# Expert rounds of a perceiver layer: tables in turn order, the tail of the down projection on half the rows, and part of its loading on ACT

## The reference

```python
x = x + cross_attention(layernorm(x), ctx_2048, mask)     # 256 tokens x 512, memory of 4096 rows
x = x + self_attention(layernorm(x), w_qkv, w_out, q_gain) # 16 heads of 32, causal, rotary on even heads
# expert layer, on layernorm(x):
router_logits = x @ gate_w                                 # 64 experts
routing_weights, selected = jax.lax.top_k(router_logits, 8)
routing_weights = jax.nn.softmax(routing_weights, axis=-1)
gate = ragged_dot(hidden_sorted, gate_proj_w, group_sizes) # per expert 512 x 192
up   = ragged_dot(hidden_sorted, up_proj_w, group_sizes)   # per expert 512 x 192
down = ragged_dot(silu(gate) * up, down_proj_w, group_sizes) # per expert 192 x 512
out  = sum over the 8 chosen experts of down * routing_weight
```

## Time and profile before

| what | value |
|---|---|
| time, median of 3 runs | 379.88 us (377.63 to 380.1) |
| time of the profiled execution | 380.15 us |
| span of that execution, first to last instruction | 378.4 us |
| PE busy | 323.2 us (85%) |
| DVE, ACT, POOL busy | 166.6, 119.3, 85.3 us |
| rounds (Silu instructions) | 28, in 16 teams |
| first gate and up product | at 149.79 us |

### The profile page before, as it was taken

How to read it: one execution, slowest core, us unless ns; L and a number is a source line. 1 busy time by engine, 2 the same in 40 slices (tenths; PEclk the granted TensorE clock), 3 DMA queues, 4 the chain that set the end, 5 groups by cost and what they waited for, 6 DMA issues and landing times.

```text
span 378.4 us, 9715 instructions
## 1 busy us (share of the span) xinstructions
PE 323.2 (85%) x3092; PEld 184.3 (49%) x3093; DVE 166.6 (44%) x450; ACT 119.3 (32%) x190; POOL 85.3 (23%) x376
## 2 busy tenths in 40 slices
PE   0699999889967524998999999998999999999894
PEld 0554444447743413445555555554654555555462
DVE  7733565945856770133233333333333332333233
ACT  1112202154731401143334433343333433333431
POOL 4000003200000003222243224423342322422320
PEclk9999999995989655799999999999999999999999
DMA  2999959100000039002999805993993999999501
GB/s 60 357 403 408 408 188 377 40 3 0 2 2 0 0 113 388 1 0 76 363 356 382 325 0 185 396 390 112 381 381 153 337 383 392 394 387 396 205 0 55
DMA packets 39743, 83.22 MB, mean 220 GB/s; under 512 B 4648, under 2 KB 12976, under 8 KB 39600
## 3 DMA queue, kind: packets, MB, share of 16 engines
q1 hardware_dynamic: 39312, 82.99, 58.5%
q10 hardware_dynamic: 416, 0.04, 0.1%
HBM read 82.49 MB, written 0.52 MB: 219 GB/s over the span
## 4 chain that ended last, share of the span: by engine, by line
PE 53%; DVE 12%; POOLq 11%; issue 9%; POOL 8%; ACT 4%; DVEq 2%; ACTq 0%
PE psum L1076 12%; POOLq L489 7%; PE psum L1131 6%; PE psum L1109 6%; PE psum L906 4%; PE psum L945 4%; PE psum L918 4%; PE psum L1084 3%; POOL store L496 3%; POOL store L501 3%; POOLq L490 2%; DVE store L728 2%; PE psum L1118 2%; POOL store L505 2%; PE psum L1006 2%
## 5 line engine op out<-in xcount | busy, mean ns | idle before, releaser
L1109 PE MATMUL psum<-store 128*32 128x384 f32 x896 | 80.0, 499 | 0.7 <-ACT store L856 0.7
L1076 PE MATMUL psum<-store 128*128 128x128 bf16 x696 | 45.9, 222 | 18.6 <-DVE store L728 18.2
L1076 PEld LDWEIGHTS psum<-store 128*128 128x128 bf16 x696 | 40.9, 99 | 38.8 <-DVE store L728 25.6
L496 POOL TENSOR_TENSOR store<-store,slot_row 128x64 f32<-128x64 f32 x112 | 29.5, 295 | 123.4 <-issue 120.4
L1131 PE MATMUL psum<-store 128*32 128x256 f32 (+1 forms) x672 | 54.0, 454 | 0.0
L501 POOL TENSOR_TENSOR store<-store 128x64 f32<-128x64 bf16 x112 | 29.5, 295 | 96.5 <-PE psum L1118 95.9
L1109 PEld LDWEIGHTS psum<-store 128*32 128x32 f32 x896 | 29.2, 112 | 39.9 <-issue 34.7
L873 ACT ACTIVATE y_parts<-psum,w_slot 128x512 fp32r<-128x512 f32 x28 | 19.2, 687 | 77.7 <-PE psum L1131 77.7
L1084 PE MATMUL psum<-y_parts,place_T 128*128 128x512 f32 x120 | 36.0, 423 | 4.1 <-DVE y_parts L711 2.5
L868 ACT ACT_TABLE_LOAD x28 | 35.9, 1283 | 7.1 <-issue 6.9
L856 ACT ACTIVATE store<-psum 128x512 f32<-128x512 f32 x29 | 17.3, 598 | 61.2 <-PE psum L1076 61.2
(11 more groups left out here) (207 smaller groups left out, 357.6 us busy)
## 6 DMA issues: line engine op xcount, KB each, us to landing
store<-n_L_ffn_gate_proj_w_dram SPq DMA_DIRECT2D x64, 384.0 KB, 5.7
store<-in_L_ffn_up_proj_w_dram SPq DMA_DIRECT2D x64, 384.0 KB, 6.0
store<-n_L_ffn_down_proj_w_dram SPq DMA_DIRECT2D x64, 256.0 KB, 5.7
store<-n_L_ffn_down_proj_w_dram SPq DMA_DIRECT2D x64, 128.0 KB, 5.9
store<-in_L_attn_w_qkv_dram SPq DMA_DIRECT2D x1, 3072.0 KB, 14.4
store<-in_ctx_dram SPq DMA_DIRECT2D x2, 1024.0 KB, 6.3
store<-in_L_attn_w_out_dram SPq DMA_DIRECT2D x1, 1024.0 KB, 16.5
x_sb<-in_x_dram SPq DMA_DIRECT2D x1, 512.0 KB, 4.3
```

Of the source, the lines that this page charges most:

```text
L496: last = pool.tensor_tensor(apart[:, :, j], over_slots(rank, e), slots, ALU.subtract)
L1076: last = pe.matmul(bank[3][:, c * P:(c + 1) * P], xparts[:, h, part, c, :], pick_t[:, h], start=(k == 0), stop=(k == 3 * TH - 1))
L1109: last = pe.matmul(bank[0][quarter, 0:2 * INTER], xs[:, c, quarter], w[:, :, c, :], start=(c == 0), stop=(c == DC - 1))
```

## The change

- `rank` and `rw` are carried over into turn order by a product with the turn table (`turned`), so POOL does L496 and L501 in one instruction each for a whole team and loads no expert numbers; `slot_no` has the slot numbers of all rounds, so that L505 goes. Teams 0 to 2 use the tables as they are.
- Hidden values of the tail stand once for each half: rows 0 to 63 of the tail's place hold the left columns, rows 64 to 127 the right ones. Down is four groups of products of 256 columns: main left, main right, tail left (rows 0 to 63 of the array), tail right (rows 64 to 127). Left goes to bank 6, right to bank 7. One transpose fewer, and 256 instead of 384 columns to copy to `hidT`.
- The tail is thus two DMAs an expert, five in all. For teams 4 to 15 SP issues four of them, and ACT issues the right tail: after the last round of team q - 4 it loads the expert number from `turns` and issues the DMA, four times, before it goes on to the next team.
- PE takes the rounds of a team out of two packed words by shift and mask, instead of a load for each team.
- One Silu on a single value (`warm`) ahead of the loop.
- Ahead of the loop: clearing is done at the program's start, the subtractions for the bfloat16 parts move from DVE to POOL, the router works by halves of the tokens, the routing weights are computed before the order of the experts, and the first gather takes its own `pick_0` from DVE and runs before the lists are made.

```diff
-        hid = carve([P, 3 * P + 2])
-        hid_tails = hid[:, P:].rearrange("p (h n) -> p h n", h=2)[:, :, 0:P:2]
-        hidT = carve([P, 3, P])
+        hid = carve([P, 2 * P])
+        hid_tails = hid[:, P:].rearrange("p (h n) -> p h n", h=2)
+        hidT = carve([P, 2, P])
...
+        y_half = (psum[:, 6, D // 2:], psum[:, 7, 0:D // 2])
+        y_whole = psum[:, 6:8, :].rearrange("p b n -> p (b n)")[:, D // 2:D // 2 + D]
...
+        def tail_of(lane, e, half):
+            cols = slice(half * (D // 2), (half + 1) * (D // 2))
+            return (lane[half * TAIL_I:(half + 1) * TAIL_I, TAIL_AT:SLOT_W],
+                    down_proj[bass.ds(e, 1), MAIN_I:, cols].rearrange("e r n -> (e r) n"))
...
-                                     (lane[:, TAIL_AT:SLOT_W], down_proj[bass.ds(e, 1), MAIN_I:].rearrange("e r (h n) -> (e r h) n", h=2))):
+                    for dst, src in parts + [tail_of(lane, e, half) for half in range(tails)]:
                         sp.dma_start(dst, src).then_inc(s_w[r], 16)
...
-                load_team(team, r)
+                load_team(team, r, tails=1)
...
-            pool.wait_ge(s_tables, 12)
-            pool.wait_ge(s_cnt, 2)
+            for part, ready, done in ((0, s_xp1, s_xr1), (1, s_xp2, s_xp)):
+                for h in range(TH):
+                    pool.wait_ge(ready, h + 1)
+                    if part == 0:
+                        pool.tensor_tensor(rest[:, h], xn[:, h].rearrange("p (q c) -> p c q", c=DC),
+                                           xparts[:, h, 0], ALU.subtract).then_inc(done, 1)
+                    else:
+                        pool.tensor_tensor(xparts[:, h, 2], rest[:, h], xparts[:, h, 1], ALU.subtract).then_inc(done, 1)
+
+            pool.wait_ge(s_tables, 11)
             pool.wait_ge(s_rk, 1)
             pool.wait_ge(s_rw, 1)
+            pool.wait_ge(s_cnt, 2)
             step = pool.alloc_register("pool_step")
             pool.reg_mov(step, 0)
-            slots = slot_row[:, :].unsqueeze(1).to_broadcast([P, TH, BLK])
-
-            def over_slots(table, e):
-                return table[:, :, bass.ds(e, 1)].to_broadcast([P, TH, BLK])
-
-            with pool.Fori(0, TEAMS) as q:
-                team = [pool.value_load(turns[0:1, bass.ds(q * TEAM + j, 1)], min_val=0, max_val=EXP_N - 1) for j in range(TEAM)]
+
+            def rounds_of(q, table):
                 count = pool.value_load(rounds[0:1, bass.ds(q, 1)], min_val=1, max_val=TOK // BLK)
-                with pool.Fori(0, count):
+                cols = bass.ds(q * TEAM, TEAM)
+
+                def over_slots(t):
+                    return t[:, :, cols].unsqueeze(3).to_broadcast([P, TH, TEAM, BLK])
+
+                with pool.Fori(0, count) as r:
                     v = pool.snap(step)
+                    slots = slot_no[:, bass.ds(r, 1), :].unsqueeze(1).to_broadcast([P, TH, TEAM, BLK])
                     pool.wait_ge(s_pk, v + 1)
-                    pool.wait_ge(s_gpr, v + 1)
-                    for j, e in enumerate(team):
-                        last = pool.tensor_tensor(apart[:, :, j], over_slots(rank, e), slots, ALU.subtract)
-                    last.then_inc(s_ap, 1)
+                    pool.tensor_tensor(apart, over_slots(table[:, 1]), slots, ALU.subtract).then_inc(s_ap, 1)
                     pool.wait_ge(s_pk, v + 2)
                     pool.wait_ge(s_mtp, v + 1)
-                    for j, e in enumerate(team):
-                        last = pool.tensor_tensor(mix_t[:, :, j], pick_t[:, :, j], over_slots(rw, e), ALU.mult)
-                    last.then_inc(s_mx, 1)
-                    for j, e in enumerate(team):
-                        left = rank[:, :, bass.ds(e, 1)]
-                        last = pool.tensor_tensor(left, left, blk_c[:, :, :], ALU.subtract)
-                    last.then_inc(s_gpr, 1)
+                    pool.tensor_tensor(mix_t, pick_t, over_slots(table[:, 0]), ALU.mult).then_inc(s_mx, 1)
                     pool.reg_add(step, step, 1)
+
+            with pool.Fori(0, EARLY) as q:
+                rounds_of(q, rw_rank)
+            pool.wait_ge(s_tn, 1)
+            with pool.Fori(EARLY, TEAMS) as q:
+                rounds_of(q, turned)
...
+                dve.wait_ge(s_lg, h + 1)
+                ch.step(dve.tensor_copy(logits[:, h], bank[h][:, 0:EXP_N]))
+                ch.step(dve.max(top8[:, h], logits[:, h]))
+                dve.tensor_scalar(ntop[:, h:h + 1], top8[:, h, 0:1], -1.0, None, ALU.mult).then_inc(s_tv, 1)
+                ch.step(dve.match_replace(cut[:, h], top8[:, h], logits[:, h], LOWEST))
+                dve.tensor_tensor(chosen_b[:, h], cut[:, h], logits[:, h], ALU.not_equal).then_inc(s_ch, 1)
+
+            dve.wait_ge(s_ch, 2)
+            dve.wait_ge(s_ex, 2)
+            ch.step(dve.tensor_tensor(rexp, rexp, chosen_b, ALU.mult))
+            ch.step(dve.tensor_reduce(rsum[:, :], rexp, AX.X, ALU.add))
+            ch.step(dve.reciprocal(rsum[:, :], rsum[:, :]))
+            dve.tensor_tensor(rw, rexp, rsum[:, :].unsqueeze(2).to_broadcast([P, TH, EXP_N]), ALU.mult).then_inc(s_rw, 1)
+
             dve.wait_ge(s_rank, 1)
-            n_col, n_row = bank[2][0:EXP_N, 0:1], bank[2][0:EXP_N, EXP_N:2 * EXP_N]
+            dve.scalar_tensor_tensor(rank, bank[2][:, 0:TH * EXP_N].rearrange("p (h e) -> p h e", h=TH), 1.0,
+                                     chosen_b, ALU.add, ALU.mult).then_inc(s_rk, 1)
+            dve.wait_ge(s_tables, 11)
+            dve.wait_ge(s_rk, 1)
+            dve.tensor_tensor(pick_0, rank[:, :, 0:TEAM].unsqueeze(3).to_broadcast([P, TH, TEAM, BLK]),
+                              slot_no[:, 0:1, :].unsqueeze(1).to_broadcast([P, TH, TEAM, BLK]), ALU.is_equal).then_inc(s_pk0, 1)
...
-            dve.memset(pick_t, 0.0).then_inc(s_pk, 1)
-            dve.memset(mix_t, 0.0).then_inc(s_mtp, 1)
-            dve.memset(hid, 0.0).then_inc(s_gpr, 1)
-            dve.wait_ge(s_xp2, 2)
-            for h in range(TH):
-                dve.tensor_tensor(xparts[:, h, 2], rest[:, h].rearrange("p (q c) -> p c q", c=DC),
-                                  xparts[:, h, 1], ALU.subtract).then_inc(s_xp, 1)
-
-            dve.wait_ge(s_ex, 2)
-            ch.step(dve.tensor_tensor(rexp, rexp, chosen, ALU.mult))
-            ch.step(dve.tensor_reduce(rsum[:, :], rexp, AX.X, ALU.add))
-            ch.step(dve.reciprocal(rsum[:, :], rsum[:, :]))
-            dve.tensor_tensor(rw, rexp, rsum[:, :].unsqueeze(2).to_broadcast([P, TH, EXP_N]), ALU.mult).then_inc(s_rw, 1)
...
+            dve.tensor_copy(turns[:, :], lists[:, 0:EXP_N]).then_inc(s_cnt, 1)
+            dve.wait_ge(s_cnt, 2)
+            ch.step(dve.scalar_tensor_tensor(spare[:, :], rounds[:, :], -1.0, radix[:, :], ALU.add, ALU.mult))
+            ch.step(dve.tensor_reduce(radix[:, 0:2], spare[:, :].rearrange("p (w q) -> p w q", w=2), AX.X, ALU.add))
+            dve.tensor_copy(packs[:, :], radix[:, 0:2]).then_inc(s_cnt, 1)
...
-                    dve.tensor_copy(hidT, bank[1][:, 0:3 * P].rearrange("p (k s) -> p k s", k=3)).then_inc(s_ht, 1)
+                    dve.tensor_copy(hidT, bank[1][:, 0:2 * P].rearrange("p (k s) -> p k s", k=2)).then_inc(s_ht, 1)
...
+            act.wait_ge(s_flp, 1)
+            act.activation(flipped[0:EXP_N], bank[7][0:EXP_N, :].rearrange("p (a h t) -> p a h t", a=2, h=TH), ACT.Copy).then_inc(s_flc, 1)
             act.wait_ge(s_xg, 1)
             copy_gathered()
+            act.wait_ge(s_tnp, 1)
+            act.activation(turned, bank[6][:, 0:4 * EXP_N].rearrange("p (a h e) -> p a h e", a=2, h=TH), ACT.Copy).then_inc(s_tn, 1)
+            act.wait_ge(s_cnt, 2)
             step = act.alloc_register("act_step")
             act.reg_mov(step, 0)
-            with act.Fori(0, TEAMS) as q:
+            act.activation(warm[:, :], ntop[0:1, 0:1], ACT.Silu).then_inc(s_warm, 1)
+
+            def rounds_of(q):
                 count = act.value_load(rounds[0:1, bass.ds(q, 1)], min_val=1, max_val=TOK // BLK)
                 with act.Fori(0, count):
                     v = act.snap(step)
@@ -870,8 +892,20 @@
                     copy_gathered()
                     act.wait_ge(s_y, v + 1)
                     act.wait_ge(s_ws, v + 1)
-                    act.activation(y_parts[:, 0], bank[6], ACT.Copy, scale=w_slot[:, :]).then_inc(s_yh, 1)
+                    act.activation(y_parts[:, 0], y_whole, ACT.Copy, scale=w_slot[:, :]).then_inc(s_yh, 1)
                     act.reg_add(step, step, 1)
+
+            rounds_of(0)
+            with act.Fori(1, LAPS) as lap:
+                for r in range(RING):
+                    act.wait_ge(s_y, act.snap(step))
+                    for j in range(TEAM):
+                        e = act.value_load(turns[0:1, bass.ds((lap * RING + r) * TEAM + j, 1)], min_val=0, max_val=EXP_N - 1)
+                        dst, src = tail_of(ring[r][:, j], e, 1)
+                        act.dma_start(dst, src).then_inc(s_w[r], 16)
+                    rounds_of(lap * RING + r - EARLY)
```

(57 more changed lines are left out.)

130 lines of the change are left out of this document (60 added, 70 removed).

## The result

The changed kernel takes 400.94 us (median, 400.36 to 401.65) against 378.75 us for the kernel before in the same comparison (372.6 to 380.1): ratio 1.0675, 95% interval 1.0615 to 1.0735. The forecast was 391 us in a range of 375 to 401, so 22 us were lost where 11 were forecast. The sign and the costly part were right; the gains were put too high. The profiled execution of the changed kernel took 401.65 us, with a span of 399.6, against 380.15 and 378.4. Some executions of a kernel take over 1.5% longer than its fastest, at a lower granted clock: the times in this document are medians over all executions, the ratios and their intervals leave those out.

What follows compares the result with a forecast made beforehand. The loop was taken as bound by PE, at team changes by POOL's sequencer. From 380.15 us: -8.7 - 11.5 - 7.3 + 33 + 6 = +11.5, so 391.7; median 0.3 lower, 391 us, range 375 to 401.

Steps and rivals of the forecast that it cites:

- the costly part: ACT's loads and issues of right tails ahead of Silu, at twelve team starts: loss 33 us.
- What bounds the kernel before: Expert loop bound by PE, at team changes by POOL's sequencer, whose lateness makes the gather wait 10.6 us over 15 changes.
- Tables in turn order, -11.5 us: Team changes: POOL's four expert-number loads and L505 go, so the gather's wait goes; gain 11.5 us (10.5 to 12).
- ACT issues the right tails, +33 us: Twelve team starts: four tails at 1.22 us delay Silu to 6.1 us; 2.7 us each reach PE, 33 us lost.
- the half clock, +6: Idle PE of about 2.5 us in those twelve rounds brings half-clock stretches after about half: loss 6 us (0 to 15).
- The "45" of the prediction: Loss at ACT's block if each has one issue stall as long as SP's longest, 1.46 us: 45 us instead of 33.
- PE's round, -0.26 us times 28 = -7.3: Each loop round: one transpose less, 0.11 us, and down 0.15 us shorter with tails side by side; gain 7.3 us.
- Ahead of the loop, -8.7 us: Router to first gate and up: work moved off DVE and POOL starts it at 141.1 instead of 149.8; gain 8.7 us.
- The table load: The 1.28 us load before Silu leaves the loop through the early Silu; gain nothing in rounds of before.
- the rival that priced it at 15 us: Table load stays in the loop, between ACT's issues and Silu: 12 x 1.28 = 15 us more, 406 us; chance 0.05.
- Weights "aren't late": Expert weight loads in the loop: asked for earlier than before, never late, so ACT's issues buy nothing.

Runs made afterwards that it cites:

- experiment 1: The changed kernel with ACT's block of loads and issues deleted, SP issuing all five loads of an expert: 376.82 us, ratio 0.9996.
- experiment 7: The changed kernel with 16 idle products of 256 columns on PE ahead of the wait for hidden values in every round: 421.20 us, ratio 1.122.
- experiment 6: The kernel before, with only ACT issuing its single tail DMA for teams 4 to 15, SP the other three loads: 404.50 us, ratio 1.078.
- experiment 3: The changed kernel with down's order main left, tail left, tail right, main right: 402.62 us, ratio 1.060.
- experiment 8: The changed kernel with the old single tail, all loads on SP, start clears moved to DVE's wait before the rotary part, DVE counts from packed words: 357.76 us.
- experiment 4: The changed kernel without the Silu on `warm` ahead of the loop: 401.26 us, ratio 1.062.
- experiment 11: The changed kernel with old tail layout, late clears, all loads on SP, the tail in two DMAs for partitions 0 to 63 and 64 to 127: 373.99 us.
- the twelfth: The changed kernel with the old single tail, late clears, all loads on SP, gate weights in two DMAs over 128 partitions each: 367.85 us, ratio 0.979.
- experiment 2: The changed kernel with all loads on SP and the tail as before: one DMA, three transposes, down as 512 + 256 + 256 columns: 363.92 us.
- fifth: The kernel of experiment 2, with ACT still doing the wait and four loads of expert numbers but issuing no DMA: 365.39 us, ratio 0.968.

## Why the prediction was right and wrong

- **What bounds the kernel before:** right; POOL's loads vanish from the chain, and the gather's wait with them.
- **Tables in turn order, -11.5 us:** nearly right. Beyond 26 rounds of 7.39 us each, the kernel before spends 12.4 us at its changes of team. The changed one without ACT's block (its other rounds, and the late ones of experiment 1) spends 2.7, so the gain is 9.7 us, and up to 0.9 more lies in the first round and the last.
- **ACT issues the right tails, +33 us, and the half clock, +6:** right. Predicted 1.22 us a tail, measured 1.26; Silu at 6.1 us, measured 5.5 to 6.65; 2.7 us reaching PE, measured 28.4/12 = 2.4; half clock 6 us, by experiment 7 it is 7.7. Together 39 predicted, 38.3 measured (experiment 1); that the sum is so near is in part luck, as the wait is 4.6 us less than forecast, the clock 1.7 more, and 2.2 of the 38.3 us belong to neither. Experiment 6 shows that this part suffices. SP's longest issue, which I took to lie in the loop (1.46 us), is at 24.64 us, during the attentions; in the loop it is 1.31. The "45" of the prediction would be 43.
- **PE's round, -0.26 us times 28 = -7.3:** this is the step that failed. In-team rounds take 7.39 us before and 7.34 to 7.40 after, so the term is 0, or 0.03 us a round at best. Both halves of my reasoning on the array came true, and the sum was still wrong: all eight products of the tails run side by side (they start within 0.05 us), each change of shape costs its 0.11 us (the tails, and in experiment 3 main right behind them, start that much late), and a transpose is gone. What I left out is what PE's sequencer does meanwhile: the loop's end, which the old down had hidden, now stands open for 0.2 to 0.3 us a round. I had noted that down "runs straight into gate and up" and took it for a property of the loop; it was one of the old down. Experiment 3, with 7.15 us a round, is close to the 7.39 - 0.26 = 7.13 that I had forecast: the gain exists, but in another order of the same products. The rule of the Trainium skill's "TensorEngine Tiling (Array Packing)", Tiling Modes, that a change of tiling mode drains TensorE pointed the right way. Neither it nor the 0.11 us that I took for such a drain tells of the sequencer.
- **Ahead of the loop, -8.7 us:** from the layer norm's output to the first gate and up it is 24.3 us before (125.52 to 149.79 on the timeline) and 16.06 after (127.18 to 143.24), a gain of 8.2. The term was right, but the start as a whole gained 6.55, since that output is 1.66 us later. The clears that moved to the start were costed at nothing, and they were not hidden: DVE's lane there is full, so the first layer norm starts at 7.83 instead of 6.56 us, 1.27 later. With the clears elsewhere (experiment 8) it starts at 6.54. The changed kernel:

```profile
1.21 0.27 DVE L541 MEMSET place_T<- 128x256 f32 x1
1.64 0.91 DVE L542 MEMSET y_parts<- 128x1024 f32 x1 [0.16 <-issue]
...
7.83 0.67 DVE L421 BATCH_NORM_STATS2 stats<-x_sb 128x6 f32<-128x512 f32 x1
```

  The first layer norm of the kernel before, on its own timeline:

```profile
6.56 0.67 DVE L402 BATCH_NORM_STATS2 stats<-x_sb 128x6 f32<-128x512 f32 x1
```

  The other 0.4 us are two differences that the change doesn't account for and that nearly cancel: the cross attention took 2.4 us longer in this execution, and the self-attention 2.0 us less, as it has 3.4 us at half clock less than the one before (last section).

- **The table load:** none in the loop, as forecast; but the rival that priced it at 15 us had no ground (experiment 4).
- **Weights "aren't late":** true of the changed kernel, but only because ACT takes part of the issues. I had concluded that issuing from ACT buys nothing; experiment 1 shows that it buys SP's keeping up, as rounds 25 to 27 take 41.5 us there and 28.5 with ACT's issues. And I didn't look at where the two tail loads write, which costs some 10% of the rate (experiment 11).

The miss of 10 us is thus 7.3 of PE's round, 2.1 of the start, 0.9 of the tables, 0.3 outside the span, less 0.7 of the block. Of the 2.1, 1.3 are the clears.

## What to carry to other kernels

A DMA issue is an instruction of the engine that issues it: with the load of its address it took 1.26 us here, and four of them ahead of the first operation that other engines wait for cost 38 us in twelve rounds, while the same four behind that operation cost 5. Ask of a saved product or instruction not only how long the array works, but what the sequencer hid beside it; put a change of the array's shape where the sequencer has nothing else to do. Keep a load over all 128 partitions, count the issues that an engine needs in a period against the period, and look for what stands in a lane before moving even a clear into it.

## What the hardware showed that I had not expected

- PE's sequencer reached the loop's end 0.1 us after down began with one shape of the array, 1.0 us after with the 64-row products last, and 0.64 us with them in the middle: each time with two shapes, just as the 64-row products started. It waited at the change to them and not at the change back. Some 0.2 to 0.3 us a round when nothing follows them.
- Four tiles of 64 x 32 on rows 0 to 63 and four on rows 64 to 127 start within 0.05 us of each other and take as long as four.
- Loads into 64 partitions (64 KB each): 340 to 375 GB/s over all in the full queue against 380 to 400, with 11% of the bytes in them. SP's issues of down's weights took 471 ns in the median in the eleventh kernel, 381 in the twelfth.
- A PE idle for 1.9 to 2.8 us in a round of 10 us is followed by a stretch at 1.2 GHz in five rounds of twelve, and the three longest of these idle times (2.65 to 2.78 us) are not among the five.
- Where a table load stands depends on how the loops are cut. In the kernel before, whose 28 rounds are one nest of loops, L868 has one in every round. With team 0 ahead of the nest (experiments 4 and 6) there are three, in its three rounds, and none in the 25 that follow, which are entered with the table in place.
- The time to the first gate and up differs between kernels whose code ahead of it is the same, but for the tails' loads and one clear in the second and fifth (143.2, 143.0, 138.6 and 141.2 us in the changed kernel and experiments 1, 2 and 5). The larger part is the clock. Every trace but that of experiment 2 has 10.2 us at half clock in the self-attention, from 82 to 86 us on; it takes 61.9 to 62.2 us with them and 57.7 without (from the last layer norm ahead of it to the first behind it), and 63.8 to 64.0 in the four traces (before, experiments 1, 7 and 12) with 3.4 us more at about 112 us. Another 2 us lie in the cross attention, which takes 38.5 to 38.9 us in the changed kernel and experiments 2 to 4 and 36.1 to 36.8 in the ten others; its first eight products of 512 columns take 5.4 to 5.8 us in these four instead of 3.7 to 3.9. Why it is so in these executions stays open.
